# Node blocks worked inside the edge loops of a three-layer graph kernel, instead of in node stages of their own

## What is computed

```python
# convolution: gather the source rows, weight them, sum per destination, multiply per node
h = relu(layernorm(x)) @ W_lin1 * z ;  w = silu(edge_attr_8 @ fc_w0) @ fc_w1
y = segment_sum(products of w, h[src], edge_attr_4, dst)
x1 = x + c_s * (h_in @ W_sc) + c_x * (y @ W_lin2) * z
hT = relu(layernorm(x1))
# each of two GAT layers, from z = hT @ W, el = z.al, er = z.ar
e = leaky_relu(el[src] + er[dst]);  ex = exp(e - segment_max(e)[dst])
out = segment_sum(ex * z[src], dst) / segment_sum(ex, dst)
hT = elu(out + hT + b)
# result: hT of the second GAT layer + x1
```

## Time and profile before

| what | value |
|---|---|
| device time, median of 3 runs | 3744.23 us (3743.74 to 3749.36) |
| the profiled execution | 3746.37 us, of which the span of its instructions is 3744.5 us |
| engines busy, share of the span | PE 75%, DVE 58%, ACT 43%, POOL 67% |
| indirect gathers (POOL) | 832 per layer, mean 0.98 us each |
| HBM traffic | 387.6 MB read, 57.3 MB written, 119 GB/s over the span |

### The profile page before, as it was taken

The page is one execution under the profiler, slowest core; times in us unless marked ns, Lnnn a source line. Parts: engine busy times, 40 slices in busy tenths (PEclk is TensorE's granted clock), DMA queues, the critical chain, the costliest instruction groups (busy, mean ns, idle before and its releaser), DMA issues. The chain is left out here.

```text
span 3744.5 us, 104678 instructions
## 1 busy us (share of the span) xinstructions
PE 2798.1 (75%) x34012; PEld 2160.8 (58%) x34012; DVE 2188.3 (58%) x6860; ACT 1622.8 (43%) x6321; POOL 2506.0 (67%) x2547
## 2 busy tenths in 40 slices
PE   3676777777777967777777777786777777777778
PEld 2454544544445856666666666654666666666655
DVE  6577777667666745555555555564555555555547
ACT  4522222222221445555555555554555555555545
POOL 3377777777777157777777777605777777777750
PEclk9889888888898865555555555576565555555555
DMA  6633333333333644444443434354444444434437
GB/s 205 200 106 105 106 106 105 105 106 105 105 105 104 214 147 107 106 107 107 107 107 106 107 106 106 95 170 133 107 107 107 106 107 107 107 107 107 106 81 222
DMA packets 259038, 445.90 MB, mean 119 GB/s; under 512 B 85597, under 2 KB 164881, under 8 KB 258843
## 3 DMA queue, kind: packets, MB, share of 16 engines
q0 software_dynamic: 119808, 334.13, 32.3%
q1 hardware_dynamic: 139171, 111.06, 10.0%
HBM read 387.62 MB, written 57.34 MB: 119 GB/s over the span
## 5 line engine op out<-in xcount | busy, mean ns | idle before, releaser
L1341 POOL DMA_INDIRECT nodes<-z_rows,scratch x1664 | 1640.1, 986 | 637.5 <-issue 462.6
L844 POOL DMA_INDIRECT scratch<-h_rows,scratch x832 | 811.9, 976 | 329.9 <-issue 326.0
L1320 ACT ACTIVATE scratch<-scratch 128x32 f32<-128x32 f32 x3328 | 727.8, 306 | 6.7
L1416 PE MATMUL ge_part<-nodes,scratch 128*32 128x64 f32 x13312 | 449.9, 314 | 178.3 <-DVE scratch L1556 176.5
L1416 PEld LDWEIGHTS ge_part<-nodes,scratch 128*32 128x32 f32 x13312 | 355.5, 168 | 219.8 <-issue 210.2
L891 PE MATMUL ce_part<-nodes,scratch 128*32 128x128 f32 (+1 forms) x6656 | 335.6, 353 | 196.2 <-DVE nodes L940 193.5
L891 PEld LDWEIGHTS ce_part<-nodes,scratch 128*32 128x32 f32 x6656 | 212.7, 127 | 314.1 <-DVE nodes L940 224.2
L940 DVE TENSOR_TENSOR nodes<-ce_w,scratch 128x768 f32<-128x768 f32 x416 | 377.0, 948 | 0.0
L871 PE MATMUL ce_w<-fc_sb,scratch 64*128 64x256 f32 x1664 | 272.9, 452 | 84.4 <-ACT scratch L815 84.4
L1325 ACT COPY scratch<-ge_part 128x260 f32<-128x260 f32 x208 | 78.0, 375 | 588.2 <-PE ge_part L1421 588.2
L938 DVE TENSOR_TENSOR nodes<-ce_w,scratch 128x512 f32<-128x512 f32 x208 | 143.8, 691 | 295.1 <-DMA scratch<-h_rows,scratch 257.5
(11 more groups left out here) (199 smaller groups left out, 5218.7 us busy)
## 6 DMA issues: line engine op xcount, KB each, us to landing
nodes<-z_rows,scratch POOLq DMA_INDIRECT x1664
z_rows<-scratch SPq DMA_DIRECT2D x52, 264.0 KB, 2.3
scratch<-x SPq DMA_DIRECT2D x52, 256.0 KB, 3.8
scratch<-h_rows,scratch POOLq DMA_INDIRECT x832
hT<-scratch SPq DMA_DIRECT2D x52, 256.0 KB, 2.2
scratch<-hT SPq DMA_DIRECT2D x52, 256.0 KB, 2.8
h_rows<-scratch SPq DMA_DIRECT2D x26, 256.0 KB, 3.0
x_skip<-scratch SPq DMA_DIRECT2D x26, 256.0 KB, 3.4
```

The source lines that it names most:

```text
L844: nc.gpsimd.indirect_dma_start(xg[u][:, i * D:(i + 1) * D], None, m.h_rows, bass.IndirectOffsetOnAxis(ap=idx[r][:, k:k + 1], axis=0)).then ...
L1320: ins = nc.scalar.activation(weighted(k, h), one_hot(r, k), ACT.Copy, scale=ex[u][:, h * (G + 1) + k:h * (G + 1) + k + 1])
L1341: nc.gpsimd.indirect_dma_start(zg[r][:, k * ZW:(k + 1) * ZW], None, m.z_rows[layer], bass.IndirectOffsetOnAxis(ap=idx[r][:, k:k + 1], axis ...
L1416: ins = nc.tensor.matmul(ps_part[j * TW:(j + 1) * TW, h * HF:(h + 1) * HF], weighted(k, h), zg[r][:, k * ZW + h * HF:k * ZW + (h + 1) * HF ...
```

## The change

The two functions of a layer become one, `conv_stage` and `gat_stage`. In each quad one block of 256 nodes whose sums are final is worked, with single buffers and one PSUM bank (`ps_node`), its pieces spread over the four steps; a short loop after the quads works the blocks left. Setup computes three tables from the window bases: which block a quad takes, the first block left over, and an offset (`lead`) that keeps the semaphore counts in line. A quad with no new final block works the spare block 25. For this input's bases, 23 of 25 real blocks fall inside the quads, 3 of the 26 quads take the spare block, and 2 blocks are left for the loop.

Also changed: `hidden` is one matmul of 512 columns on 16 rows (before: two of 256 columns on two row groups at once), with one `ea8` buffer and one DMA per step; `ps_er4` moves into the bank of `ps_runs`, with an added wait for `init_ready`; in the GAT step `place_er` now runs before `finish_tiles` on DVE; denominators are no longer sent through DRAM, each quad does its own max and reciprocal on 4 partitions; the semaphore clean-up moves from behind the input stage to behind the convolution; the node stages' barriers are gone. The zeroing of the convolution's columns moves from POOL (L1042) to DVE.

Convolution, SP:

```diff
+            def load_x(n, k):
+                sp.wait_ge(s_h, k + 1)
+                sp.wait_ge(st_x1, k * 16 + 16)
+                sp.dma_start(tile(node.x), rows_of(m.x_skip, n)).then_inc(x_in, 16)
...
+                if r == 0:
+                    slot.n = load_block(sp, m, quad)
+                    load_x(slot.n, quad)
                 if ahead >= 2:
-                    sp.wait_ge(hid_ps, v + 1)
-                    load(v + 2, r % 2)
+                    sp.wait_ge(hid_ps, v + 2)
+                    load(v + 2)
+                if r == 1:
+                    store_x1(slot.n, quad)
+                if r == 2:
+                    store_hT(slot.n, quad)
+                if r == 3:
+                    store_rows(slot.n, quad)
```

Convolution, ACT:

```diff
             def step(quad, r, ahead):
                 v = quad * 4 + r
+                if r == 2:
+                    hidden_state(quad)
+                if r == 3:
+                    rows(quad, 0)
                 if ahead >= 1:
                     silu(v + 1, (r + 1) % 2)
                 act.wait_ge(unit_summed, v * 2 + 4)
                 nc.scalar.copy(sums, ps_part[:, :]).then_inc(sums_ready, 1)
+                if r == 1:
+                    deviation_of(quad)
+                if r == 2:
+                    copy_hT(quad)
                 if ahead >= 4:
                     stage(v + 4, r)
+                if r == 3:
+                    rows(quad, 1)
```

Convolution, PE:

```diff
+            def hidden(v):
+                pe.wait_ge(ea8_in, v * 16 + 16)
+                nc.tensor.matmul(ps_hid[:, :], m.fc0[:, :], ea8, start=True, stop=True).then_inc(hid_ps, 1)
...
+                if r == 3:
+                    table(quad, 0)
                 tile_sums(v, u, 0)
                 if ahead >= 1:
-                    hidden(v + 1, 1 - u, quad * 64 + ((r + 1) // 2 + 1) * 32)
+                    hidden(v + 1)
                     weights(v + 1, 1 - u, 0)
+                if r == 2:
+                    transposes(quad)
                 tile_sums(v, u, 1)
                 if ahead >= 1:
                     weights(v + 1, 1 - u, 1)
                 window_sums(v, u)
+                if r == 0:
+                    outputs(quad)
+                if r == 3:
+                    table(quad, 1)
```

Convolution, DVE:

```diff
                 products(v, r, 0, gathered)
                 add_window(v - 1)
+                if r == 0:
+                    fixed(slot.n, quad, quad * 4 + 2)
+                if r == 1:
+                    state(slot.n, quad)
                 if ahead >= 1:
                     one_hots(v + 1, (r + 1) % 4)
                 products(v, r, 1, gathered)
                 if ahead >= 1:
                     scaled_one_hots(v + 1, (r + 1) % 4)
-
+                if r == 1:
+                    scales(quad)
```

GAT, ACT, behind the copy L1325:

```diff
                 if ahead >= 3:
                     copy_hotT(v + 3)
+                if r == 1:
+                    exponential(quad)
+                if r >= 2 and layer == 0:
+                    rows(quad, r - 2)
```

GAT, PE:

```diff
                 tile_sums(v, r, 1).then_inc(part_summed, 1)
+                if r == 0:
+                    spread(quad)
+                if r >= 2 and layer == 0:
+                    table(quad, r - 2)
+                if r == 2 and layer == 1:
+                    to_rows(quad)
                 if ahead >= 3:
                     transpose_hot(v + 3, (r + 3) % 4)
+                    pe.wait_ge(init_ready, v + 2)
                     block_er(v + 3, (r + 3) % 4, quad * 16 + (16 if r == 0 else 32))
```

GAT, DVE:

```diff
+                if r == 0:
+                    slot.n = load_block(dve, m, quad)
                 base = load_base(dve, m, v - 1)
...
                 add_window(v - 1, 1 - u, base)
+                if r == 0:
+                    denominators(slot.n, quad, quad * 4 + 2)
+                if r == 2:
+                    elu(quad)
+                if r == 3 and layer == 1:
+                    output(quad)
                 if ahead >= 3:
                     one_hots(v + 3, (r + 3) % 4)
                 node_picks(v, r)
                 if ahead >= 1:
                     into_tiles(v + 1, 1 - u)
-                    finish_tiles(v + 1, 1 - u)
                 if ahead >= 3:
                     place_er(v + 3)
+                if ahead >= 1:
+                    finish_tiles(v + 1, 1 - u)
                 if ahead >= 2:
                     scores(v + 2, (r + 2) % 4, quad * 128 + (128 if r < 2 else 256))
                 if ahead >= 1:
                     differences(v + 1, 1 - u)
+                if r == 0:
+                    node_state(slot.n, quad)
...
             add_window(last, 1, base)
+            first, lead = load_rest(dve, m, last_quad)
+            with dve.Fori(first, REAL) as n:
+                k = n + lead
+                denominators(n, k, last_quad * 4 + 6)
+                node_state(n, k)
+                elu(k)
```

645 lines of the change are left out of this document (320 added, 325 removed).

## The result

The changed kernel takes 3804.24 us (median of 4 runs, 3801.91 to 3805.35), the kernel before, run beside it, 3745.72 (3743.74 to 3749.36). The ratio is 1.0162, 95% interval 1.0149 to 1.0174: slower by 1.6%. The forecast was 3797 us. The profiled execution has a span of 3802.1 us, against 3744.5 before.

A forecast was written before the change was run, and what follows sets the result against it. POOL's issue of gathers was taken to pace the edge stages, with 0.85 us a GAT step of room. 3746.4 - 238 + 57 + 146 + 88 = 3799 profiled, 2.1 above the median, so 3797 us; range 3750 to 3850.

The forecast's parts named there:

- The chain of 9.47 us a GAT step: GAT step through PE and DVE without gather waits: 9.47 us, leaving 0.85 us a step under POOL's pace.
- Layer 0, 47.0 a quad: First GAT layer's edge loop: 47.0 us a quad, 5.6 over POOL's 41.4, times 26 is +146 (+70 to +175).
- Spread and loop's head: GAT, per quad: spread on PE behind the tile sums 2.0 us, register loads and loop's head 0.9.
- Exponential: GAT, ScalarE's three passes in r = 1, ahead of the staging: 1.3 us a quad on the chain.
- Tables less the rising clock: First GAT layer, r = 2 and 3: table halves 3.8 us a quad, less 1.0 for stretches at 2.4 GHz.
- Layer 1, 44.6: Second GAT layer's edge loop: 44.6 us a quad, 3.4 over 41.2, times 26 is +88 (+40 to +110).
- The convolution, 43.2 and +57: Convolution's edge loop: steps summing to 39.7 us a quad plus 3.5 for the low clock, 2.2 over POOL's 41.0.
- the rival with the low clock in all four steps: Convolution falls to the low clock: 49.2 us a quad for 41.0, run at 3953 us; chance 0.08.
- Savings, 238: Three stretches without gathers shrink to drain, two serial blocks and next start, saving 84, 80 and 74 us.
- the 45 to 55 us that I had named as the sign: In the profile after, the stretches without gathers would stand at 45 to 55 us.
- The table switch: Convolution, r = 2: 1.28 us for Sqrt's table load; rival 2.66 a switch, 3833 us, chance 0.04.
- Gathers stay the pace: Rival, all edge stages: the 2.2 us of DVE waiting is true room, run at 3533 us; chance 0.15.

The follow-up runs named there:

- e9: Changed kernel with GAT spread's two matmuls issued twice and two idle matmuls starting the convolution's step 2; chip 4, 5767.61 us, ratio 1.0588 to the kernel before.
- e5: Changed kernel with GAT exponential moved to ScalarE's idle time in step 2, the convolution's reciprocal, hidden_state and transposes moved into step 2; 3703.14 us, ratio 0.9894.
- e6: Changed kernel with GAT place_er moved behind differences and the convolution's scaled one-hot product made by four operations; chip 6, 3806.45 us, ratio 1.0162.
- e8: Changed kernel with e5's moves, and GAT spread, first table half or to_rows, and node_state put where their engines wait; chip 4, 5435.41 us, ratio 0.9976.
- e7: Changed kernel with e5's moves, place_er behind differences and TensorE's block matmuls behind block_er; chip 6, 3702.81 us, ratio 0.9889.

## Why the prediction was right

The forecast was 3797 with its own range of 3750 to 3850, the measured time 3804. The mechanism is the one forecast: the engines' own chain is only 0.8 us a step under the gathers' pace, so most of the node work is paid inside the edge loops, and that is more than the stretches without gathers give back. The sizes erred on both sides.

- **The chain of 9.47 us a GAT step**, and so the room of 0.85 under POOL's pace: 9.53 in layer 1's step 3. This term decided the sign; the 2.2 us of waiting in the earlier trace rows were mostly not room.
- **Layer 0, 47.0 a quad**: 46.52, and +120.3 for +146. Some 11 us of the difference are the first two quads, whose gathers run at 40.6 and 41.8 us on a lead of staged work; most of the rest is the 0.5 a quad. *Spread and loop's head*: 2.0 and 0.9 forecast, 3.54 measured for step 0. The spread is whole (e9, on chip 4), and the head costs 1.2 in layer 1 and 1.5 in layer 0, by DVE's loop turn and two register loads. *node_state*: 2.1 forecast, 1.36 measured, for the register load ahead of `scale_first`, which shows 0.71 in other steps, runs beside it. *Exponential*: 1.3 forecast, 0.77 measured (e5). *Tables less the rising clock*: 3.8 - 1.0 forecast, 1.46 and 1.28 measured, 2.7 together. Both parts are as forecast. Each half delays the next matmuls by 1.92 us, but behind it TensorE's clock is higher and what follows is shorter (rows below).
- **Layer 1, 44.6**: 44.04, and +65.1 for +88: step 0 3.27, step 1 1.03, `to_rows` 0.91 (as forecast), exponential 0.72. Some 9 us of the difference are the first three quads.
- **The convolution, 43.2 and +57**: 44.2 in mid-stage and +77.8. The steps were 9.2, 10.9, 11.0 and 8.6 before the 3.5 for the clock. At the high clock the rows show 10.21, 10.69, 10.06 and at most 11.23, so 42.2 or less for 39.7, and at least 2.0 for the clock. Step 0 was mis-sized by 1.0 and step 3 by up to 2.6; the 3.5 for the clock made up for part of it. That the convolution would be bound by the chain through DVE, not by its gathers, e5 and e6 show. The 49.2 of the rival with the low clock in all four steps is a slip: it adds 4 x 2.05 to the pace of 41.0, where the chain of 39.7 gives 47.9.
- **Savings, 238**: 206, with 56.5, 68.4 and 53.7 us left for 47.5, 53 and 45. This is the largest miss, all of one sign, and most of it is the drain, the time from the last gather to the last window added. I took it from the kernel before, 10.3, 20.6 and 20.6; in the changed kernel it is 17.6, 31.7 and 27.4, 25 us more in all. Where the chain binds, the gathers run ahead of it, so more work is left when the last of them ends. It is the same lead that shortens the first quads. The blocks in series and the ends are only some 9 us longer than worked out. Two of the three stretches lie above the 45 to 55 us that I had named as the sign.
- **The table switch**: 1.28 as the ACT row had it. The 2.66 of the Trainium skill (ScalarE: Activation LUTs, "What ACT_TABLE_LOAD costs") would have given 3833.
- **Gathers stay the pace**: refuted by DVE's 28.6 us, and the part of it on collisions by e6: the gathers did grow, by 62 us in the convolution alone, and cost nothing, since the chain bound.

The rows for the clock behind a table half: layer 0's step 3, then the same step of layer 1, which has no table.

```profile
1876.98 2.13 PE L1560 MATMUL ge_node<-wz,nodes 128*128 128x264 f32 x4
1878.90 0.63 PE L1465 MATMUL ge_hotT<-ident,scratch 128*128 128x128 f32 x2
...
1879.61 0.94 PE L1541 MATMUL ge_sum<-scratch 128*128 128x128 f32 x4
```

```profile
3029.37 1.20 PE L1541 MATMUL ge_sum<-scratch 128*128 128x128 f32 x4
```

The granted clock is 0.84 from 1879.6 to 1881.3 and 0.50 from 3029.4 to 3031.6. Over the whole edge stretch it is 0.57 in layer 0 and 0.51 in layer 1.

In the time, the savings were short by 32 and the convolution by 21, and the GAT layers were put 26 and 23 too long, so that 4 us remain. That the total came out 7 us off is partly luck. The lead of the gathers was left out on both sides, some 20 us at the starts of the GAT stages and 25 at the ends, and these cancel; the other terms are good to between a tenth and a third.

Open stay three things: what e8's GAT loops do where the kernel before takes 3745 us; how much of the convolution's loss beyond the 2.0 us a quad is the clock, since step 3 is never seen at the high clock throughout; and what it is in chips 4, 5 and 10 that makes TensorE wait.

## What to carry to other kernels

Waits before a transfer that sets the pace are not room. Take one step of the loop, replace those waits by nothing, and follow queue by queue what then ends last: that number minus the pace is all that can be hidden. Work moved into a loop from behind it costs most of its length if it goes into the in-order queue of the engine on that ring, even at a place where another engine waits; put it ahead of an existing wait of its own engine, and keep a wait for a square root or its table load out of the queue of an engine that others follow. Look also at what the old pace hid (here a loop turn and two register loads at the loop's head): it comes back as soon as the pace is lost. And do not take the drain behind the last transfer from a loop that waited for its transfers: once the engines set the pace, the transfers run ahead, and the drain grows (here by 7 to 11 us a stage).

## What the runs showed of the hardware that I had not expected

- The same program took 3742 us on chip 6 and 5436 to 5456 on chips 4, 5 and 10 (1.45 to 1.46 times). On chip 4 a matmul of L1527 was as long as elsewhere (311 ns for 313), but TensorE was idle with nothing shown to wait for, 307.8 us at L1527, 272.0 at L1532 and 213.9 at L1500, and the granted clock showed 0.60 to 0.62 in the mean of a run on these chips, for 0.65 to 0.67. Orders of the same kernels differed too: TensorE's matmuls behind `block_er` gave 50 and 72 us there, and nothing in e7.
- A table load began 0.02 us behind one ScalarE operation and let the next begin 0.01 us behind its end, 1.28 us in all. In the GAT stages it stands in each of the 25 turns of the first layer's loop and in none of the second's, in the kernel before as in the changed one.
- A gather's 0.95 us stretched to 1.9 when it began with a DVE product of 1.2 us. Cutting the product in four took 45.3 us off the gathers of a stage, and gave back 48.3 as waits.
- Two table halves a quad in layer 0 raised TensorE's granted clock behind them: 0.57 over the stage for 0.52 before, and 1.1 us a quad less than their own 2 x 1.92.
